# Gated feed-forward: square roots behind a step's evictions, attention's sums one group per step and three ahead, router and weighing in another order

## The chip, the cores and the metric
One core of a Trainium2 chip runs the whole program in one launch. The metric is device time in microseconds, the median of several runs. TensorE (PE) does the matrix products, VectorE (DVE) and ScalarE (ACT) the element-wise work, GpSimd (POOL) issues indirect transfers and SyncE (SP) plain ones.

## The reference, cut to what matters
A graph of 6250 nodes with 256 features passes through two message-passing layers and two feed-forward layers, each on the normalized rows and added to them. The change touches the second of the four:

```python
x = x + gnn0(layernorm(x), edge_attr, src, dst)                 # attention
x = x + ffn0(layernorm(x))                                      # this stage
x = x + gnn1(layernorm(x), src, dst)
x = x + ffn1(layernorm(x))

def ffn0(x):
    all_out = _experts_mlp(x, eW1, eb1, eW2, eb2, eW3, eb3)     # 4 experts, 256-128-64-256
    shared = _shared_mlp(x, sW1, sb1, sW2, sb2, sW3, sb3)       # 256-256-128-256
    gates = softmax(x @ gW + gb)
    topv, topi = top_k(gates, 2)
    topw = softmax(topv)
    gated = sum of the two chosen experts' outputs, weighed by topw
    return shared + gated
```

## The kernel before, in words
The program runs in phases; the function `gated_experts` is one of them, between attention and the second graph layer. It holds all rows in `GX` as 49 blocks of 128 rows and works on 25 groups of `GT` = 2 blocks (the last has one). Each engine has a hand-written list of work: `first` for the start and `rest` for every group g, unrolled, so each engine's order is the order of the code, and semaphores tie them.

Before a block can be used, attention's sums, which lie transposed in `ACC`, are added: PE transposes them into `pY` (`attended` on PE, L1982), DVE adds a bias (L1721) and `pY` (L1724) to the block. Then the block is normalized: `row_stats` (L243), `center` (the aggregates L1704 and the copy of the means L1706), a square root on ScalarE (`root`, L1902), its reciprocal on DVE (`scale`, L1739). Before the change sums are added in chunks of `YC` = 4 blocks, two chunks in `first` and one in each of the steps 0 to 10, and the roots are taken in five growing parts.

A step g then does, on PE: the first layers of the shared net (S1) and the experts (E1) from `xT`, in accumulations that rotate over three banks `pM`; `weights` (L2010, the transposition of the gate weights); `turn` (L1991, the transposition of the next group's rows); the second layers (S2, and the experts' `halves`, L2036); the spreading of the gate weights to `pW` (L2059) and the output's biases to `pO` (L2065); the next group's router `logits` (L2002); the last layers into `pO` (L2074, L2079). ScalarE evicts every accumulation with a bias and a Relu (`mid`, L1939), evicts `turn` into `xT` (L1884) and takes the exponentials of the router (L1891) and of the difference of its two best values (L1896). The roots and the exponentials use different function tables, and `ACT_TABLE_LOAD` brings one in.

DVE normalizes (`normed`, L1780), weighs (`weigh`, L1813 to L1819, then the copy of `wT`, L1823), multiplies the experts by their weights (`e2w`, L1853), picks the two best experts (`gates`, L1788 to L1806, nineteen small operations, with ScalarE's exponential in between) and adds the output to the block (L1862). The finished blocks are normalized once more for the next layer, in eight `pieces`: means and variances on DVE, a root (`kept`, L1908), `keep` (L1746, L1749, L1755), the scaled rows on ScalarE (`row_out`, L1917) or DVE, and POOL scatters them (L1693).

What sets the order around the change, on ScalarE at the head of a step before:

```python
for r in range(2, len(parts)):
    if g == chunk_end(r) - 1:
        root(r)
for n, (i0, i1) in enumerate(pieces):
    if i1 == g * GT:
        kept(n)
...
for n in range(KD):
    mid(n, h1[:, n, 0:w], B1[:, n:n + 1])
```

Of the kernel before, what the change touches and what calls it, by code (L numbers as in the profile page):

```python
# [21 lines left out]
ALU = mybir.AluOpType  # L22
# [22 lines left out]
PW = D + 3  # L45
# [1562 lines left out]
def gated_experts(nc, sb, ps, sem, sems, x, ACC, IDI, XND, F, x_in, bi_in, GX, ST, MEAN, RSTD, ident, iota, epsc, SORTD):  # L1608
# [3 lines left out]
    YC = 2 * GT  # L1612
    NY = (RB + YC - 1) // YC
    NGR = (RB + GT - 1) // GT
    parts = [(0, YC), (YC, 2 * YC), (2 * YC, 4 * YC), (4 * YC, 8 * YC), (8 * YC, RB)]
# [8 lines left out]
    def chunk_end(r):  # L1624
        return (parts[r][1] + YC - 1) // YC - 1

# [4 lines left out]
    with ExitStack() as s:  # L1631
# [20 lines left out]
        NMR = sb(s, "NMRk", [128, RB])  # L1652
        g_ = {n: sb(s, f"gate_{n}", [128, GT, NG]) for n in ("l", "p", "eq", "m1", "q", "w")}
# [19 lines left out]
        with nc.Block() as block:  # L1673
# [26 lines left out]
            def _(dve):  # L1700
# [8 lines left out]
                def attended(q, j):  # L1709

                    i0 = q * YC + j * GT
                    w = min(GT, RB - i0)
                    if w <= 0:
                        return
                    for n, (a, b) in enumerate(XPARTS):
                        if a == i0 or a == i0 + 1:
                            dve.wait_ge(x_in[n], 16 * (b - a))
                    if i0 == 0:
# [3 lines left out]
                    dve.wait_ge(yt_ready, i0 // GT + 1)  # L1722
# [12 lines left out]
                def scale(r):  # L1735

                    dve.wait_ge(r_ready, r + 1)
                    i0, i1 = parts[r]
                    nc.vector.reciprocal(RSTD[:, i0:i1], SD[0][:, i0:i1])  # L1739
                    dve.drain()  # L1740
# [67 lines left out]
                def weigh(g, k):  # L1808
                    w = width(g)
                    one = g_["w"][:, 0:w, :]  # L1810
                    dve.wait_ge(ex_ready, g * 2 + 2)

                    nc.vector.tensor_scalar(r_["f"][:, 0:w], r_["e"][:, 0:w], 1.0, None, ALU.add)  # L1813
                    nc.vector.tensor_tensor(one, one, spread(r_["e"], w), ALU.mult)
                    dve.drain()
                    nc.vector.reciprocal(r_["f"][:, 0:w], r_["f"][:, 0:w])
                    nc.vector.tensor_tensor(one, one, g_["m1"][:, 0:w, :], ALU.add)
                    dve.drain()
                    nc.vector.tensor_tensor(GWP[:, 0:w, 0:2, 0:NG], one.unsqueeze(2).to_broadcast([128, w, 2, NG]),  # L1819
                                            r_["f"][:, 0:w].unsqueeze(2).unsqueeze(3).to_broadcast([128, w, 2, NG]),  # L1820
                                            ALU.mult).then_inc(w_ready, 1)
                    dve.wait_ge(wt_ready, g + 1)
                    nc.vector.tensor_copy(wT[k][:, 0:w * 128], pG[0:WROW + NG + 1, 256:256 + w * 128]).then_inc(wt_copied, 1)  # L1823

                def first(g, k):
                    nc.vector.memset(GWP[:, :, :, :], 0.0)
                    nc.vector.tensor_scalar(IDE[:, :], iota[:, 0:NG], -1.0, float(NG), ALU.mult, ALU.add)
                    dve.drain()
                    nc.vector.memset(GWP[:, :, 1, NG], 1.0)
                    for j in range(2):  # L1830
                        attended(0, j)
                    measured(0)
                    scale(0)
                    normed(g)
                    gates(g)
                    for j in range(2):
                        attended(1, j)
                    measured(1)

                def rest(g, k, more):  # L1840
                    w = width(g)
                    for r in range(1, len(parts)):
                        if g == chunk_end(r):
                            scale(r)
                    if more:
                        normed(g + 1)
                    weigh(g, k)
                    if g + 2 < NY:
                        attended(g + 2, 0)
# [11 lines left out]
                    v = block_of(GX, g * GT, w)  # L1861
                    nc.vector.tensor_tensor(v, v, pO[:, 0:w * D].rearrange("p (m d) -> p m d", d=D), ALU.add).then_inc(o_read, 1)  # L1862
                    dve.drain()
                    for m in range(w):
                        row_stats(nc, ST, GX, g * GT + m, PW)
                    if g + 2 < NY:
                        measured(g + 2)
                    for n, (i0, i1) in enumerate(pieces):
                        if i1 == g * GT:
                            keep(n)  # L1870
                        if i1 == min((g + 1) * GT, RB):
                            dve.drain()
                            center(i0, i1, MV[1]).then_inc(kc_ready, 1)
                            if not more:
                                keep(n)
# [4 lines left out]
            def _(act):  # L1880
# [17 lines left out]
                def root(r):  # L1898

                    act.wait_ge(c_ready, chunk_end(r) + 1)  # L1900
                    i0, i1 = parts[r]
                    nc.scalar.activation(SD[0][:, i0:i1], MV[0][:, i0:i1, 1], ACT.Sqrt, bias=epsc[:, :]).then_inc(r_ready, 1)  # L1902

                def kept(n):

                    act.wait_ge(kc_ready, n + 1)
                    i0, i1 = pieces[n]
                    nc.scalar.activation(SD[1][:, i0:i1], MV[1][:, i0:i1, 1], ACT.Sqrt, bias=epsc[:, :]).then_inc(kr_ready, 1)  # L1908

# [12 lines left out]
                def first(g, k):  # L1922
                    root(0)
                    normed(g, k)
                    exp_gates(g)

                def rest(g, k, more):
                    w = width(g) * 128
                    for r in range(2, len(parts)):
                        if g == chunk_end(r) - 1:  # L1930
                            root(r)
                    for n, (i0, i1) in enumerate(pieces):
                        if i1 == g * GT:
                            kept(n)

# [18 lines left out]
                    if g == 0:  # L1954
                        root(1)
# [10 lines left out]
            def _(pe):  # L1966
# [6 lines left out]
                def attended(q, j):  # L1973

                    i0 = q * YC + j * GT
                    if i0 >= RB:
                        return
                    if i0:
                        pe.wait_ge(y_read, i0 // GT)
                    for m in range(min(GT, RB - i0)):  # L1980
                        for c in range(KD):
                            last = nc.tensor.transpose(pY[:, m * D + c * 128:m * D + (c + 1) * 128],  # L1982
                                                       acc[:, c, (i0 + m) * 128:(i0 + m + 1) * 128], ident[:, :])
                    last.then_inc(yt_ready, 1)
# [29 lines left out]
                def first(g, k):  # L2014
                    for j in range(2):
                        attended(0, j)
                    turn(g)
                    logits(g, k)
                    for j in range(2):
                        attended(1, j)  # L2020

                def rest(g, k, more):
# [16 lines left out]

                    if g + 2 < NY:  # L2040
                        attended(g + 2, 0)
# [5 lines left out]
                    if more:  # L2047
                        turn(g + 1)

# [17 lines left out]
                    if g + 2 < NY:  # L2067
# [620 lines left out]
```

## Time and profile before

| | before |
|---|---|
| median of 3 runs | 3106.71 us (3104.43 to 3108.81) |
| the profiled execution's own time | 3102.67 us |
| its span | 3100.9 us |
| busy: PE, DVE, ACT, POOL | 75%, 56%, 41%, 59% of the span |
| this stage, from its first to the next phase's first work | 1248.4 to 1701.2 us |
| busy in the stage: PE, DVE, ACT | 356.1, 232.9, 180.8 of 452.8 us |

The span is the time between the first and the last instruction of one profiled execution; the shares are means over phases with different limits, so the stage is read by itself. DVE's busy time counts its operations, not the drains between dependent ones.

### The profile page before, as it was taken

What the parts mean: (1) busy time and instruction counts of PE and PEld (TensorE: products, weight loads), DVE (VectorE), ACT (ScalarE), POOL (GpSimd) and SP (SyncE); (2) the same over time, 40 slices, a digit from 0 to 9 for tenths busy, and PEclk for the clock granted to TensorE, in tenths of its full rate; (3) what the DMA queues carried; (4) which work ended last, traced back from release to release, by engine and by line L of the source; (5) the groups of instructions that cost most, each with busy time, mean ns of one, the idle gap of its engine ahead of it and who ended that gap; (6) DMA issues with size and microseconds to landing.
All of it is one profiled execution on the core that took longest, in us unless ns stands there. A gap on an engine that the chain in (4) does not pass through costs nothing. (4 is left out here: it accounts for less than half of the span.)

```text
span 3100.9 us, 46865 instructions
## 1 busy us (share of the span) xinstructions
PE 2331.6 (75%) x12072; PEld 1959.1 (63%) x12072; DVE 1741.5 (56%) x5674; ACT 1273.4 (41%) x4542; POOL 1837.1 (59%) x1935
## 2 busy tenths in 40 slices
PE   5986667667666666688894787888888888875098
PEld 4876666666666566566773676666666666764087
DVE  5434888898888887566452433333333333476154
ACT  1534555555555444333543433333333333353033
POOL 5575777777777775501122777777777777400645
PEclk8998788888888878798996656555555556687599
DMA  7698444444444453600001333333333333203242
GB/s 208 178 230 218 110 111 112 113 112 111 113 113 111 113 128 85 207 1 14 14 28 36 106 106 106 106 106 106 106 106 106 106 106 106 66 1 53 99 140 83
DMA packets 250114, 323.65 MB, mean 104 GB/s; under 512 B 152723, under 2 KB 181001, under 8 KB 249335
## 3 DMA queue, kind: packets, MB, share of 16 engines
q0 software_dynamic: 89424, 235.59, 27.1%
q1 hardware_dynamic: 155784, 82.05, 11.1%
q10 hardware_dynamic: 4640, 3.02, 0.5%
q8 instruction: 100, 1.64, 0.2%
q14 instruction: 166, 1.36, 0.1%
HBM read 276.41 MB, written 48.24 MB: 105 GB/s over the span
## 5 line engine op out<-in xcount | busy, mean ns | idle before, releaser
L1526 PE MATMUL pAb<-HOTb,Gb 128*128 128x128 f32 x3136 | 840.8, 425 | 173.3 <-DMA Gb<-normed_rows,SRCT 122.0
L1505 POOL DMA_INDIRECT Gb<-normed_rows,SRCT x784 | 741.2, 945 | 248.9 <-issue 238.5
L1526 PEld LDWEIGHTS pAb<-HOTb,Gb 128*128 128x128 f32 x3136 | 659.7, 297 | 354.8 <-DMA Gb<-normed_rows,SRCT 273.9
L1566 DVE TENSOR_TENSOR ACC<-ACC,pAb 128x256 f32 x784 | 330.6, 422 | 641.7 <-PE pAb L1526 568.6
L1093 POOL DMA_INDIRECT GX<-ft_rows,SRCT x432 | 412.3, 954 | 131.5 <-issue 130.9
L1179 ACT ACTIVATE ACC<-apA 128x254 f32 x784 | 300.4, 383 | 411.5 <-PE apA L1252 339.9
L1252 PE MATMUL apA<-AHOT,GX 128*128 128x129 f32 x1920 | 304.8, 329 | 84.2 <-DVE GX L1401 84.2
L1252 PEld LDWEIGHTS apA<-AHOT,GX 128*128 128x128 f32 x1920 | 290.5, 241 | 101.9 <-DVE GX L1401 101.9
L1545 ACT ACTIVATE HOTb<-OFFb 128x1024 f32<-128x1024 f32 x98 | 103.6, 1057 | 604.1 <-PE pAb L1526 604.0
L1093 POOL DMA_INDIRECT G<-ft_rows,SRCT x288 | 274.6, 954 | 87.6 <-issue 85.4
L1693 POOL DMA_INDIRECT normed_rows<-nrow,IDI x49 | 48.1, 981 | 338.8 <-ACT nrow L1917 325.4
L1541 ACT ACTIVATE OFFb<-iota,NRELb 128x128 f32<-128x128 f32 x784 | 239.6, 388 | 6.9 <-issue 0.3
L1252 PE MATMUL apA<-AHOT,G 128*128 128x129 f32 x1216 | 197.9, 335 | 48.2 <-DVE G L1401 46.4
L1252 PEld LDWEIGHTS apA<-AHOT,G 128*128 128x128 f32 x1216 | 189.4, 247 | 59.0 <-DVE G L1401 56.9
L1401 DVE TENSOR_TENSOR GX<-GX,apV 128x1024 f32<-128x1024 f32 x120 | 143.1, 1192 | 0.0
L1180 ACT ACTIVATE FL<-apA 128x4 f32<-128x4 f32 x784 | 135.1, 172 | 0.0
L2298 POOL DMA_INDIRECT rows_by_expert<-GX,POSI x49 | 48.6, 992 | 135.5 <-DVE POSI L2485 120.9
L2029 PE MATMUL fpM<-fxT,ffn_E 128*128 128x256 f32 (+1 forms) x400 | 103.4, 414 | 33.5 <-ACT h L1939 33.5
L2546 POOL DMA_INDIRECT out_dram<-sO,sID x80 | 77.7, 972 | 76.2 <-issue 41.5
L1301 DVE TENSOR_TENSOR AHOT<-apL,RELT 128x1024 f32<-128x1024 f32 x98 | 118.6, 1210 | 0.0
L2029 PEld LDWEIGHTS fpM<-fxT,ffn_E 128*128 128x128 f32 x400 | 82.9, 213 | 49.8 <-ACT h L1939 37.3
L520 PE MATMUL pS<-VB,eT 128*128 128x128 f32 x784 | 97.7, 279 | 0.5 <-ACT V L617 0.5
(415 smaller groups left out, 3954.2 us busy)
## 6 DMA issues: line engine op xcount, KB each, us to landing
ebuf<-in_edge_attr_dram SPq DMA_DIRECT2D x49, 448.0 KB
Gb<-normed_rows,SRCT POOLq DMA_INDIRECT x784, 2.7
rows_by_expert<-ffn_PADT SPq DMA_DIRECT2D x1, 10360.0 KB, 44.8
sT<-rows_by_expert SPq DMA_DIRECT2D x80, 129.5 KB, 2.1
GX<-ft_rows,SRCT POOLq DMA_INDIRECT x480
ft_rows<-row SPq DMA_DIRECT2D x25, 231.0 KB
GX<-in_x_dram SPq DMA_DIRECT2D x10, 560.0 KB
G<-ft_rows,SRCT POOLq DMA_INDIRECT x304
```

Source lines behind the costliest of these rows:

```text
L1093: pool.indirect_dma_start(G[c % GS][:, m, :], None, FT[:, :], bass.IndirectOffsetOnAxis(ap=SRCT[:, t:t + 1], axis=0)).then_inc(g_in[c % GS ...
L1179: nc.scalar.activation(acc[:, :, ds(r + 1, EP - 1)], sums[:, :, 1:EP], ACT.Copy)
L1180: nc.scalar.activation(FL[:, :, f:n + 1:n - f], sums[:, :, 0:HW:EP], ACT.Copy).then_inc(pfree[b], 1)
L1252: last = nc.tensor.matmul(pA[b][:, f * HW:(f + 1) * HW], G[c % GS][:, m, f * 128:(f + 1) * 128], HOT[c % 2][:, m, :], start=True, stop=True)
L1301: nc.vector.tensor_tensor(HOT[c % 2][:, h * HT:(h + 1) * HT, 0:EP], pL[0:EP, 256:256 + EP].unsqueeze(1).to_broadcast([EP, HT, EP]), RELT[: ...
L1401: nc.vector.tensor_tensor(v, v, pV[0:EP, 0:128].rearrange("p (h m) -> p h m", m=UT)[:, :, m:m + WB].rearrange("p h m -> p m h").unsqueeze( ...
L1505: pool.indirect_dma_start(G[g % R][m][:, :], None, TABLE[:, :], bass.IndirectOffsetOnAxis(ap=SRCT[:, t:t + 1], axis=0)).then_inc(g_in[g % ...
L1526: last = nc.tensor.matmul(pA[b][:, o:o + EP], G[k][m][:, c * 128:(c + 1) * 128], HOT[k % 2][:, m, :], start=True, stop=True)
L1541: nc.scalar.activation(OFF[k2][:, m, :], iota[0:EP, 0:EP], ACT.Abs, bias=NREL[k2][:, m:m + 1])
L1545: nc.scalar.activation(HOT[k2][:, :, :], OFF[k2][:, :, :], ACT.Relu, bias=1.0, scale=-1.0).then_inc(hot[k2], 1)
L1566: last = nc.vector.tensor_tensor(acc[:, :, ds(b, EP)], acc[:, :, ds(b, EP)], pA[q][:, o:o + KD * EP].rearrange("p (c r) -> p c r", c=KD), ...
L2029: last = nc.tensor.matmul(pM[bank[n]][:, 0:w], one, v, start=(c == 0), stop=(c == len(pairs) - 1))
```

## The change
Attention's sums are added one group (two blocks) per step, with statistics, aggregates and the copy of the means at once; in step 0 the groups 2 and 3, in step g the group g + 3. The parts of the roots follow: one group, one group, then two groups each. The roots (`root`, `kept`) move from the head of a step on ScalarE to its end, behind the evictions and the next group's exponential, and a dummy exponential on one element (`exp_next`) follows them. The second exponential comes behind the first expert's eviction. On DVE weighing comes ahead of normalizing, the copy of `wT` is parted from it, the output is added at the end of a step and its statistics are taken in the next one (`settled`). On PE the sums' transposes and the logits move ahead of the experts' second layers.

The tables:

```diff
+    AHEAD = 3
+    parts = [(0, 1), (1, 2)] + [(g, min(g + 2, NGR)) for g in range(2, NGR, 2)]
+    coming = [[2, 3]] + [[g + AHEAD] if g + AHEAD < NGR else [] for g in range(1, NGR)]
```

On DVE:

```diff
-                def measured(q):
-
-                    i0, i1 = q * YC, min((q + 1) * YC, RB)
-                    dve.drain()
-                    for i in range(i0, i1):
+                    dve.drain()
+                    for i in range(i0, i0 + w):
                         row_stats(nc, ST, GX, i, PW)
                     dve.drain()
-                    center(i0, i1, MV[0]).then_inc(c_ready, 1)
+                    last = center(i0, i0 + w, MV[0])
+                    if any(q == b - 1 for a, b in parts):
+                        last.then_inc(c_ready, 1)
...
                 def rest(g, k, more):
                     w = width(g)
-                    for r in range(1, len(parts)):
-                        if g == chunk_end(r):
+                    weigh(g, k)
+                    for r, (a, b) in enumerate(parts):
+                        if a == g + 1:
                             scale(r)
                     if more:
                         normed(g + 1)
-                    weigh(g, k)
-                    if g + 2 < NY:
-                        attended(g + 2, 0)
+                    for n, (i0, i1) in enumerate(pieces):
+                        if i1 == (g - 1) * GT:
+                            keep(n)
+                    if g:
+                        settled(g - 1)
+                    dve.wait_ge(wt_ready, g + 1)
+                    nc.vector.tensor_copy(wT[k][:, 0:w * 128], pG[0:WROW + NG + 1, 256:256 + w * 128]).then_inc(wt_copied, 1)
+                    for q in coming[g]:
+                        attended(q)
...
-                    if g + 2 < NY:
-                        attended(g + 2, 1)
                     if more:
                         gates(g + 1)
-                    dve.wait_ge(o_ready, g + 1)
...
+                    else:
+                        keep(len(pieces) - 2)
+                    added(g)
+                    if not more:
+                        settled(g)
+                        keep(len(pieces) - 1)
```

On ScalarE:

```diff
                 def rest(g, k, more):
                     w = width(g) * 128
-                    for r in range(2, len(parts)):
-                        if g == chunk_end(r) - 1:
-                            root(r)
-                    for n, (i0, i1) in enumerate(pieces):
-                        if i1 == g * GT:
-                            kept(n)
...
-                        if e == 1:
+                        if e == 0:
                             exp_second(g)
...
                     if more:
                         exp_gates(g + 1)
-                    else:
+                    due = 0
+                    for r, (a, b) in enumerate(parts):
+                        if r >= 2 and b - 1 in coming[g]:
+                            root(r)
+                            due += 1
+                    for n, (i0, i1) in enumerate(pieces):
+                        if i1 == g * GT:
+                            kept(n)
+                            due += 1
+                    if not more:
                         kept(len(pieces) - 1)
+                    elif due:
+                        exp_next()
```

On PE:

```diff
-                    if g + 2 < NY:
-                        attended(g + 2, 0)
...
                     weights(g)
                     if more:
                         turn(g + 1)
+                    for q in coming[g][0:1]:
+                        attended(q)
...
                     mid(KD + NG, [(S2[:, c, :], h1[:, c, 0:w]) for c in range(KD)])
+                    pe.wait_ge(wt_copied, g + 2)
+                    if more:
+                        logits(g + 1, 1 - k)
                     for b in range(NB):
                         halves(KD + NG + 1 + b, b)
-                    pe.wait_ge(wt_copied, g + 2)
...
-                    if g + 2 < NY:
-                        attended(g + 2, 1)
-                    if more:
-                        logits(g + 1, 1 - k)
+                    for q in coming[g][1:2]:
+                        attended(q)
```

How the instructions stand before and after, engine by engine (line, operation, output <- inputs, shape, how many in a row). ScalarE around a root of the kept rows, before:

```order
L1939 ACTIVATE e<-fpM,ffn_C 128x256 x2
L1891 ACTIVATE gate_p<-gate_l 128x8
L1908 ACT_TABLE_LOAD
L1908 ACTIVATE SDm<-MVm,epsc 128x8
L1939 ACTIVATE h<-fpM,ffn_B 128x256 x2
L1939 ACTIVATE e<-fpM,ffn_C 128x256 x2
L1896 ACT_TABLE_LOAD
L1896 ACTIVATE gred_e<-gred_d 128x2
L1939 ACTIVATE e<-fpM,ffn_C 128x256 x2
```

and around a root now:

```order
L1939 ACTIVATE e<-fpM,ffn_C 128x256 x2
L1893 ACTIVATE gate_p<-gate_l 128x8
L1904 ACT_TABLE_LOAD
L1904 ACTIVATE SDm<-MVm,epsc 128x4
L1914 ACT_TABLE_LOAD
L1914 ACTIVATE spare<-epsc 128x1
L1939 ACTIVATE h<-fpM,ffn_B 128x256 x2
L1939 ACTIVATE e<-fpM,ffn_C 128x256
L1898 ACTIVATE gred_e<-gred_d 128x2
```

The load and the root stood ahead of the first evictions (`h`, `e`), with a second load inside the evictions; now load, root, load and dummy stand behind the next group's exponential (`gate_p`), and the second exponential (`gred_e`) comes one eviction earlier.

DVE from the adding of a group's output to the copy of `wT`, before (step 1 to step 2):

```order
L1862 TENSOR_TENSOR GX<-GX,fpO 128x2x256
L243 BN_STATS ST<-GX 128x6 x6
L1704 BN_AGGR MVm<-ST 128x2 x4
L1706 COPY MEAN<-MVm 128x4
L1780 TENSOR_SCALAR fxn<-GX,MEAN,RSTD 128x256 x2
L1813 TENSOR_SCALAR gred_f<-gred_e 128x2
L1814 TENSOR_TENSOR gate_w<-gate_w,gred_e 128x8
L1816 RECIPROCAL gred_f<-gred_f 128x2
L1817 TENSOR_TENSOR gate_w<-gate_w,gate_m 128x8
L1819 TENSOR_TENSOR gate_rows<-gate_w,gred_f 128x2x2x4
L1823 COPY wT<-fpG 37x256
```

and now (from step 0 into step 1, up to the first add of attention's sums):

```order
L1824 TENSOR_TENSOR GX<-GX,fpO 128x2x256
L1809 TENSOR_SCALAR gred_f<-gred_e 128x2
L1810 TENSOR_TENSOR gate_w<-gate_w,gred_e 128x8
L1812 RECIPROCAL gred_f<-gred_f 128x2
L1813 TENSOR_TENSOR gate_w<-gate_w,gate_m 128x8
L1815 TENSOR_TENSOR gate_rows<-gate_w,gred_f 128x2x2x4
L1735 RECIPROCAL RSTD<-SDm 128x4
L1776 TENSOR_SCALAR fxn<-GX,MEAN,RSTD 128x256 x2
L243 BN_STATS ST<-GX 128x6 x2
L1861 COPY wT<-fpG 37x256
L1719 TENSOR_TENSOR GX<-GX,ffn_BI 128x2x256
```

The statistics of six blocks and four aggregates between the output and the weighing are gone from there; the weighing (L1813 to L1819 before, L1809 to L1815 now) follows the output directly, and normalizing and two statistics come behind it.

PE from the first layers to the logits, before:

```order
L2029 MATMUL fpM<-fxT,ffn_S 128x256 x4
L2029 MATMUL fpM<-fxT,ffn_E 128x256 x8
L2010 MATMUL fpG<-ident,gate_rows 128x128 x2
L1991 MATMUL fpT<-ident,fxn 128x128 x4
L2029 MATMUL fpM<-h,ffn_S 128x256 x2
L2036 MATMUL fpM<-e,ffn_E 64x256 x4
L2059 MATMUL fpW<-wT,ffn_SEL 128x256
L2065 MATMUL fpO<-ffn_OB,wT 128x256
L2059 MATMUL fpW<-wT,ffn_SEL 128x256
L2065 MATMUL fpO<-ffn_OB,wT 128x256
L1982 MATMUL fpY<-ident,ACC 128x128 x4
L2002 MATMUL fpG<-ffn_GW,fxT 128x128 x4
```

and now:

```order
L2034 MATMUL fpM<-fxT,ffn_S 128x256 x4
L2034 MATMUL fpM<-fxT,ffn_E 128x256 x8
L2017 MATMUL fpG<-ident,gate_rows 128x128 x2
L1998 MATMUL fpT<-ident,fxn 128x128 x4
L1989 MATMUL fpY<-ident,ACC 128x128 x4
L2034 MATMUL fpM<-h,ffn_S 128x256 x2
L2009 MATMUL fpG<-ffn_GW,fxT 128x128 x4
L2041 MATMUL fpM<-e,ffn_E 64x256 x4
L2066 MATMUL fpW<-wT,ffn_SEL 128x256
L2072 MATMUL fpO<-ffn_OB,wT 128x256
L2066 MATMUL fpW<-wT,ffn_SEL 128x256
L2072 MATMUL fpO<-ffn_OB,wT 128x256
```

The sums' transposes (`fpY`) and the logits (`fpG<-ffn_GW,fxT`) stood behind the spreading of the gate weights (`fpW`); now they stand ahead of the experts' second layers.

## Rows read from the trace of the kernel before
**Rows 1.** Windows: stretch, its us, busy us (records) per engine, granted clock, DMA, GB/s.
```profile
1292.30:1664.40 372.10, 320.29 (x1674) 251.09 (x1674) 203.57 (x885) 161.92 (x343) 41.13 (x41) 0.93 0.05 16
1350.20:1365.80 15.60, 13.64 (x79) 10.89 (x78) 11.31 (x46) 5.78 (x14) 0.00 (x0) 1.00 0.00 0
1401.80:1424.20 22.40, 16.60 (x76) 12.50 (x77) 11.90 (x53) 7.95 (x16) 0.00 (x0) 0.77 0.00 0
1506.10:1518.80 12.70, 12.70 (x71) 10.02 (x71) 6.55 (x31) 6.21 (x14) 2.88 (x3) 1.00 0.12 43
1586.60:1603.40 16.80, 14.35 (x74) 10.96 (x73) 7.53 (x40) 8.87 (x18) 0.00 (x0) 0.95 0.00 1
```

**Rows 2.** Waits from 1292.3 to 1664.4: who waited, total us, times, longest.
```profile
ACT SDm L1908 <- DVE MEAN L1706: 39.5, 7, 7.2
```

**Rows 3.** Timeline (start us, us, engine, line, operation, count, idle before), step with a root.
```profile
1419.39 0.30 ACT L1908 ACTIVATE SDm<-MVm,epsc 128x8 f32<-128x8 f32 x1 [7.20 <-DVE MEAN L1706]
1420.10 4.80 PE L2029 MATMUL fpM<-fxT,ffn_E 128*128 128x256 f32 x12 [5.01 <-ACT h L1939]
1422.71 1.28 ACT L1896 ACT_TABLE_LOAD   x1
1424.00 0.20 ACT L1896 ACTIVATE gred_e<-gred_d 128x2 f32<-128x2 f32 x1
```

**Rows 4.** Timeline of PE: sums' transposes at 1428, then a step without roots or sums.
```profile
1428.83 0.66 PE L1982 MATMUL fpY<-ident,ACC 128*128 128x128 f32 x4
1429.32 1.06 PE L2002 MATMUL fpG<-ffn_GW,fxT 128*128 128x128 f32 x8
1506.92 0.44 PE L2010 MATMUL fpG<-ident,gate_rows 128*128 128x128 f32 x2
1508.76 1.08 PE L2036 MATMUL fpM<-e,ffn_E 128*64 128x256 f32 x8
1509.77 0.48 PE L2059 MATMUL fpW<-wT,ffn_SEL 4*128 4x256 f32 x1
1510.84 1.16 PE L2002 MATMUL fpG<-ffn_GW,fxT 128*128 128x128 f32 x8
1514.42 1.89 PE L2029 MATMUL fpM<-fxT,ffn_S 128*128 128x256 f32 x8
```

**Rows 5.** Timeline of DVE and ScalarE: aggregates at 1417, then that same step.
```profile
1417.76 0.38 DVE L1704 BATCH_NORM_AGGREGATE MVm<-ST 128x2 f32<-128x6 f32 x4
1506.08 0.17 DVE L1813 TENSOR_SCALAR gred_f<-gred_e 128x2 f32<-128x2 f32 x1
1507.40 0.42 DVE L1823 COPY wT<-fpG 37x256 f32<-37x256 f32 x1 [0.53 <-PE fpG L2010]
1510.94 0.69 DVE L1853 TENSOR_TENSOR e2w<-e,fpW 128x512 f32<-128x512 f32 x1 [3.12 <-PE fpW L2059]
1512.03 0.17 DVE L1788 TENSOR_TENSOR gate_l<-fpG,ffn_GBB 128x8 f32<-128x8 f32 x1 [0.41 <-PE fpG L2002]
1512.72 0.21 ACT L1891 ACTIVATE gate_p<-gate_l 128x8 f32<-128x8 f32 x1 [1.08 <-DVE gate_l L1793]
1515.49 0.47 ACT L1939 ACTIVATE h<-fpM,ffn_B 128x256 f32<-128x256 f32 x1 [2.56 <-PE fpM L2029]
1516.76 0.68 DVE L1862 TENSOR_TENSOR GX<-GX,fpO 128x512 f32<-128x512 f32 x1
1517.53 0.75 DVE L243 BATCH_NORM_STATS2 ST<-GX 128x6 f32<-128x256 f32 x2
1518.20 0.72 DVE L1780 TENSOR_SCALAR fxn<-GX,MEAN,RSTD 128x256 f32<-128x256 f32 x2
```

**Rows 6.** Timeline of PE and POOL: the stage's first and last work.
```profile
1258.64 2.07 PE L2002 MATMUL fpG<-ffn_GW,fxT 128*128 128x128 f32 x8 [0.69 <-ACT fxT L1884]
1269.52 3.62 PE L2029 MATMUL fpM<-fxT,ffn_S 128*128 128x256 f32 x8
1690.53 0.97 POOL L1693 DMA_INDIRECT normed_rows<-nrow,IDI  x1 [0.30 <-issue]
```

More of the change, by code:

```diff
@@ L1622, in gated_experts, with rows_of @@
             kept_in.setdefault(i1 // GT + 1 + (i - i0) // 2, []).append((n, i))
-    def chunk_end(r):
-        return (parts[r][1] + YC - 1) // YC - 1
+    def rows_of(a, b):
+        return slice(a * GT, min(b * GT, RB))
     def out_before(n):
@@ L1707, in center, with attended @@
                     return last
[L1709 to L1714, printed above, removed]
+                def attended(q):
+                    i0, w = q * GT, width(q)
                     for n, (a, b) in enumerate(XPARTS):
-                        if a == i0 or a == i0 + 1:
+                        if a == i0:
                             dve.wait_ge(x_in[n], 16 * (b - a))
-                    if i0 == 0:
+                    if q == 0:
                         dve.wait_ge(bi_in, 16)
@@ L1821, in weigh, with added, settled @@
                                             ALU.mult).then_inc(w_ready, 1)
-                    dve.wait_ge(wt_ready, g + 1)
-                    nc.vector.tensor_copy(wT[k][:, 0:w * 128], pG[0:WROW + NG + 1, 256:256 + w * 128]).then_inc(wt_copied, 1)
+                def added(g):
+                    w = width(g)
+                    dve.wait_ge(o_ready, g + 1)
+                    v = block_of(GX, g * GT, w)
+                    nc.vector.tensor_tensor(v, v, pO[:, 0:w * D].rearrange("p (m d) -> p m d", d=D), ALU.add).then_inc(o_read, 1)
+                    dve.drain()
+                def settled(g):
+                    for m in range(width(g)):
+                        row_stats(nc, ST, GX, g * GT + m, PW)
+                    for n, (i0, i1) in enumerate(pieces):
+                        if i1 == min((g + 1) * GT, RB):
+                            dve.drain()
+                            center(i0, i1, MV[1]).then_inc(kc_ready, 1)
                 def first(g, k):
@@ L1829, in first @@
                     nc.vector.memset(GWP[:, :, 1, NG], 1.0)
-                    for j in range(2):
-                        attended(0, j)
-                    measured(0)
+                    attended(0)
                     scale(0)
                     normed(g)
+                    attended(1)
                     gates(g)
-                    for j in range(2):
-                        attended(1, j)
-                    measured(1)
                 def rest(g, k, more):
                     w = width(g)
-                    for r in range(1, len(parts)):
-                        if g == chunk_end(r):
+                    weigh(g, k)
+                    for r, (a, b) in enumerate(parts):
+                        if a == g + 1:
                             scale(r)
@@ L1898, in root @@
                 def root(r):
-                    act.wait_ge(c_ready, chunk_end(r) + 1)
-                    i0, i1 = parts[r]
-                    nc.scalar.activation(SD[0][:, i0:i1], MV[0][:, i0:i1, 1], ACT.Sqrt, bias=epsc[:, :]).then_inc(r_ready, 1)
+                    act.wait_ge(c_ready, r + 1)
+                    o = rows_of(*parts[r])
+                    nc.scalar.activation(SD[0][:, o], MV[0][:, o, 1], ACT.Sqrt, bias=epsc[:, :]).then_inc(r_ready, 1)
                 def kept(n):
@@ L1908, in kept, with exp_next @@
                     nc.scalar.activation(SD[1][:, i0:i1], MV[1][:, i0:i1, 1], ACT.Sqrt, bias=epsc[:, :]).then_inc(kr_ready, 1)
+                def exp_next():
+                    nc.scalar.activation(spare[:, :], epsc[:, :], ACT.Exp)
                 def row_out(n, i):
@@ L1923, in first @@
                     root(0)
+                    root(1)
                     normed(g, k)
@@ L1928, in rest @@
                     w = width(g) * 128
-                    for r in range(2, len(parts)):
-                        if g == chunk_end(r) - 1:
-                            root(r)
-                    for n, (i0, i1) in enumerate(pieces):
-                        if i1 == g * GT:
-                            kept(n)
                     def mid(n, to, b):
@@ L1959, in rest @@
                         exp_gates(g + 1)
-                    else:
+                    due = 0
[3 more added lines that the diff above has]
+                            due += 1
+                    for n, (i0, i1) in enumerate(pieces):
+                        if i1 == g * GT:
+                            kept(n)
+                            due += 1
+                    if not more:
                         kept(len(pieces) - 1)
+                    elif due:
+                        exp_next()
                 unrolled(NGR, 2, lambda c, k, i: first(c, k), lambda c, k, i, more: rest(c, k, more))
@@ L1971, in _, with attended @@
                 pe.sem_inc(wt_copied, 1)
[L1973 to L1980, printed above, removed]
+                def attended(q):
+                    if q:
+                        pe.wait_ge(y_read, q)
+                    for m in range(width(q)):
                         for c in range(KD):
+                            i = q * GT + m
                             last = nc.tensor.transpose(pY[:, m * D + c * 128:m * D + (c + 1) * 128],
-                                                       acc[:, c, (i0 + m) * 128:(i0 + m + 1) * 128], ident[:, :])
+                                                       acc[:, c, i * 128:(i + 1) * 128], ident[:, :])
                     last.then_inc(yt_ready, 1)
@@ L2014, in first @@
                 def first(g, k):
-                    for j in range(2):
-                        attended(0, j)
+                    for q in range(2):
+                        attended(q)
                     turn(g)
                     logits(g, k)
-                    for j in range(2):
-                        attended(1, j)
                 def rest(g, k, more):
```

25 lines of the change are left out of this document (5 added, 20 removed).

## The prediction
> **What bounds the kernel now.** I read the windows first. The change touches one stage, the gated feed-forward, whose 25 groups of two row blocks are handled in 25 steps. I cut it where DVE begins the weighing of a group (the division by 1 + e, L1813): from the second group's weighing to the last one's are 372.1 us, that is 23 steps, 16.18 us each [rows 1]. TensorE is recorded busy for 320.3 us of that, so it looks like the bound. The windows of single steps say otherwise: a step that carries neither square roots nor attention's sums takes 12.70 us, and in it PE is busy for all of 12.70; one with roots alone takes 16.80; one with two groups of sums and no roots 15.60; one with both 22.40, at a granted clock of 0.77. PE sets only the 12.70. What is above it is waiting.
>
> Where the waiting is stands in the table of waits and the timeline. In these 23 steps ScalarE sat 39.5 us, seven times, in front of the square roots of L1908 alone until DVE had finished its means [rows 2]. ScalarE runs in order, and the evictions of the next accumulations stand behind the root. The timeline shows one: the root starts at 1419.39 after 7.20 us, and PE, out of banks, starts again at 1420.10 after 5.01 us, for 12 records that take 4.80 us, 0.40 each, where eight take 1.89, 0.24 each, at the full clock [rows 3, 4]. Then the exponential of the router's second value needs its table again (1.28 us) before DVE can weigh. The kernel alternates: DVE holds ScalarE, ScalarE holds PE, PE comes back at half speed, and DVE waits for all of them.
>
> **The root.** It now stands behind the last evictions of a step and the exponential of the next group, in the gap before the next step's first accumulation is ready, and it works on sums added three groups ahead, finished in the same step before e2w. So it waits for nothing. A dummy exponential behind it fetches the other table. I cost its place by the fast step [rows 4, 5]. PW (the spreading of the gate weights, 1509.77) starts 1.17 us before e2w (1510.94); e2w takes 0.69; the exponential ends 0.90 after the router's first instruction (1512.03 to 1512.93). Two loads, the root and the dummy are 1.28 + 0.30 + 1.28 + 0.20 = 3.06. ScalarE is free 1.17 + 0.69 + 0.90 + 3.06 = 5.82 us after PW starts. PE reaches the next accumulations 4.65 after PW (1514.42), minus 0.99 for the logits that move ahead of PW, so at 3.66, and two accumulations take 1.89. The first is ready at 4.6; it is evicted 1.2 late. But PE has three banks: the fourth accumulation, at 3.66 + 2.8 = 6.5, needs the first bank, read by 5.82 + 0.47 = 6.29. Two evictions take 0.94 and two accumulations 1.89, so ScalarE catches up. Cost: zero to 0.4 us; its cover is these three banks. Without it, a root costs its lateness of 1.2 us.
>
> Here a rule speaks against the change. The trace: the load begun at 1422.71 ends at 1423.99 and the exponential starts at 1424.00 [rows 3]; nothing is drained behind a load. The Trainium skill (ScalarE: Activation LUTs, What ACT_TABLE_LOAD costs, and its table-set sections) says to group functions by set, since a switch is about 1.28 us of load plus 1.38 of drain; the change goes from 25 loads to 29. By that page the pair above would be 2.76 us longer. The trace denies the drain, so I leave it out of the sum.
>
> **Attention's sums.** The same 49 blocks, but one group per step in steps 1 to 21 (two in step 0) instead of two in steps 0 to 10. On DVE one group is two adds (0.68, or 0.77 with the drain behind: 1516.76 to 1517.53), two statistics (0.75), two aggregates (four take 0.38) and a small copy (0.16, as L1813), with drains between of under 0.1 each: 2.7 to 2.9 us [rows 5]. On PE it is four transposes, recorded as 0.66, though the next matmuls start 0.49 after them (1428.83 to 1429.32); the same overlap of 0.17 makes the logits 0.99 of their 1.16 [rows 4].
>
> **The step's three loops.** (a) PE: the step in which it is never idle, 12.70 [rows 1], plus 0.49 to 0.66: 13.2 to 13.4. (b) DVE alone: weighing 0.84, normalizing 0.72, statistics 0.75, copy of wT 0.42, sums 2.8, e2w 0.69, gates 4.73 (1512.03 to 1516.76), adding 0.77: 11.7, and 0.3 more on average for scales, shifts and kept means. (c) Through both: weighing to PE's transposition 0.84 (1506.08 to 1506.92); up to 0.5 in which PE now waits for the normalized rows, since these come behind the weighing instead of ahead of it; transposition to PW 2.85 plus the moved transposes 0.49 to 0.66 and logits 0.99 to 1.16; PW to e2w 1.17; e2w 0.69; gates 4.73; adding 0.77. Sum 13.03 to 13.37, or 12.5 if PE is late enough not to wait for the rows. The copy of wT, behind the normalizing and statistics, ends about 2.8 after the weighing began, or 3.7 with eight kept means; PE asks for it after its second shared layer, at about 0.84 + 0.5 + 1.84 (1506.92 to 1508.76) = 3.2, plus up to 0.5 for the transposes: it waits at most 0.5, once in four steps. I take 13.3 for all: (a) and (c) nearly tie, and the odd 0.4 for a root or a late copy lies between their ends. In steps 22 and 23 no sums are left: 12.7.
>
> 23 steps: 21 x 13.3 + 2 x 12.7 = 304.7 instead of 372.1, a gain of 67.4.
>
> **Head and tail.** Now PE's first accumulations start at 1269.52, although the logits were done by 1260.71; between lie transposes that wait for DVE's sums [rows 6]. The change moves them off that path: 8.8 us earlier. Step 0 adds two groups of sums now as before, and I leave its length. In the last step six blocks are scaled (as normalizing, two in 0.72 [rows 5]: 2.2 us) ahead of the copy of wT, on which the last evictions and so the last kept rows wait; behind these POOL issues the scatters up to 1690.53. A loss of 2.2. The edits of pieces (spans of parts, the second exponential one eviction earlier) move nothing else.
>
> Sum: 8.8 + 67.4 - 2.2 = 74.0. The profiled execution took 3102.67 us; the median of the three runs, 3106.71, is 4.04 above. On the median: 3106.7 - 74 = 3032.7, rounded to **3032 us**.
>
> **Rivals.**
> *Roots still bite* (0.14). Something I don't see makes ScalarE later by two more loads' worth, 2.6 us, in each of the 12 root steps of the loop (g = 0, 2 ... 20, and 21): 31 us, 3063. For: three banks are all the cover, and steps with a root and a kept root have another 0.30. Against: the 0.01 between load and exponential. The Trainium skill's drain, above, would be this case.
> *DVE remains the pace* (0.10). Its waits stay additive, as in today's 15.60 step with sums and no roots, where PE is busy for only 13.64: 21 x 15.6 instead of 21 x 13.3 is 48 more, 3081. Against: that step carries two groups, and DVE's own sum is 11.7.
> *Slower* (0.04). The second exponential now stands behind the first expert's eviction, not the second's. If DVE finishes the gates later than that, ScalarE holds three experts' evictions, PE runs out of banks and its clock falls, as at 1420.10. It decides from the point where a step exceeds (372.1 + 6.6 - 25.4) / 21 = 16.8 us, 3.5 above my loop; at 18 us a step the time is 3107 + 25 = 3132. Against: the gates end 1.17 + 0.69 + 4.73 = 6.59 after PW starts, and that eviction ends at 3.66 + 2.8 + 0.47 = 6.9 at the earliest; behind it there are again three banks.
> My forecast has 0.72.
>
> **Range.** The forecast's own: 12.9 instead of 13.3 takes 8 off, a head better by 6 another 6: 3018; at 14.15, halfway between 12.70 and 15.60, 18 more: 3050. To hold 8 in 10 I take in the roots' case with a margin: **3015 to 3068**; left out are DVE's pace and the slower case. 0.2% is 6 us, about what a measurement of this kernel can tell from no change. Faster 0.95, same 0.02, slower 0.03: all but the slower case lie well below, and that case can end on either side of its point.
>
> **What would show it.** Right: steps of 13 to 13.5 us, alike whether they have roots or not; no wait of a root on DVE's means; PE's waits on evictions below 1 us and a granted clock of 1.00 in the loop; the second weighing at about 1283 and the last at about 1588. Wrong: PE idle behind ScalarE's evictions after root steps (first rival); e2w starting late with PE idle before the last matmuls, or DVE without idle time (second); ScalarE waiting for DVE in front of the second exponential (third).

## The result and the profile after

The changed kernel takes 3021.99 us (median of 4 runs, 3016.28 to 3026.84) against 3105.57 of before on the same chip: a ratio of 0.973 [0.971, 0.975], faster by 83.6 us. The forecast was 3032 us, 74 less. The profiled execution took 3018.93 us, its span 3017.1, 83.8 under that of before.

Windows of the changed kernel, with the columns of [rows 1] (the busy columns are PE, PE's weight loads, DVE, ScalarE, POOL): the 23 steps from the second weighing to the last one, a step behind a root, and the next one, which has a root at its end.

```profile
1280.50:1577.70 297.20, 295.64 (x1689) 242.98 (x1689) 208.11 (x909) 172.26 (x368) 51.84 (x50) 1.00 0.10 33
1436.20:1449.20 13.00, 13.00 (x76) 10.82 (x75) 9.55 (x41) 6.21 (x14) 4.72 (x5) 1.00 0.14 50
1449.20:1462.10 12.90, 12.90 (x75) 10.69 (x75) 9.06 (x38) 9.06 (x18) 0.00 (x0) 1.00 0.01 2
```

The 372.10 of [rows 1] are 297.20: 12.92 a step, alike with and without roots, PE busy in 99.5% of them at a granted clock of 1.00. Of the 74.9 us, 50.2 are idle time of PE (51.8 before, 1.6 now) and 24.7 are busy time (320.3 before, 295.6 now), as the granted clock rose from 0.93 to 1.00. Waits of the changed kernel from 1270 to 1610, as in [rows 2]:

```profile
DVE e2w L1867 <- PE fpW L2066: 33.9, 24, 4.1
ACT SDm L1910 <- DVE MEAN L1707: 12.7, 1, 12.7
DVE gred_f L1809 <- ACT gred_e L1898: 7.6, 22, 0.4
PE fpM L2034 <- ACT h L1939: 1.0, 2, 0.8
PE fpM L2041 <- DVE wT L1861: 2.2, 1, 2.2
```

The one wait of a root on means that is left is that of the very last piece, behind which no eviction stands. DVE waits for PE now, and no step's PE waits over 1 us for an eviction. The timeline from a root (L1904, L1910, the kept rows' of the same table) to the turn answers to [rows 3]:

```profile
1431.66 1.28 ACT L1904 ACT_TABLE_LOAD   x1
1432.74 1.89 PE L2034 MATMUL fpM<-fxT,ffn_S 128*128 128x256 f32 x8
1432.96 0.30 ACT L1904 ACTIVATE SDm<-MVm,epsc 128x4 f32<-128x4 f32 x1
1433.16 0.28 ACT L1910 ACTIVATE SDm<-MVm,epsc 128x8 f32<-128x8 f32 x1
1433.46 1.28 ACT L1914 ACT_TABLE_LOAD   x1
1434.47 3.77 PE L2034 MATMUL fpM<-fxT,ffn_E 128*128 128x256 f32 x16
1434.76 0.20 ACT L1914 ACTIVATE spare<-epsc 128x1 f32<-128x1 f32 x1
1434.87 0.82 ACT L1939 ACTIVATE h<-fpM,ffn_B 128x256 f32<-128x256 f32 x2
1435.94 0.21 ACT L1898 ACTIVATE gred_e<-gred_d 128x2 f32<-128x2 f32 x1
1437.13 0.95 DVE L1776 TENSOR_SCALAR fxn<-GX,MEAN,RSTD 128x256 f32<-128x256 f32 x2
1438.29 0.60 PE L1998 MATMUL fpT<-ident,fxn 128*128 128x128 f32 x4
```

Two loads, two roots and the dummy run while PE accumulates; the evictions start at 1434.87, and PE goes on at 0.24 us a record without a wait. The second exponential needs no load. The stage's head and end in the timeline, to be read beside [rows 6]:

```profile
1259.94 3.45 PE L2034 MATMUL fpM<-fxT,ffn_S 128*128 128x256 f32 x8
1264.66 0.20 ACT L1898 ACTIVATE gred_e<-gred_d 128x2 f32<-128x2 f32 x1
...
1582.11 0.66 PE L2041 MATMUL fpM<-e,ffn_E 128*64 128x128 f32 x8 [2.22 <-DVE wT L1861]
1605.65 0.97 POOL L1694 DMA_INDIRECT normed_rows<-nrow,IDI  x1 [0.30 <-issue]
```

The sum by the same cuts: the second weighing comes 12.3 us earlier against the stage's first transfer, the 23 steps take 74.9 less, the end from the last weighing to the last scatter 1.9 more (27.97 instead of 26.1). That is 85.3; the rest of the program is 1.5 longer.

### The profile page after: what moved, and what is told of

It is laid out like the page before. It is cut to its first block and busy times, and to the rows that moved or that the text cites. A ratio compares the mean times of both kernels' runs of the same rounds, so it can differ in the third digit from the quotient of the medians.

```text
span 3017.1 us, 46958 instructions
## 1 busy us (share of the span) xinstructions
PE 2261.7 (75%) x12072; PEld 1908.8 (63%) x12072; DVE 1745.5 (58%) x5695; ACT 1283.2 (43%) x4568; POOL 1837.4 (61%) x1935
## 5 line engine op out<-in xcount | busy, mean ns | idle before, releaser
L1526 PE MATMUL pAb<-HOTb,Gb 128*128 128x128 f32 x3136 | 811.5, 412 | 203.9 <-DMA Gb<-normed_rows,SRCT 154.0
L1526 PEld LDWEIGHTS pAb<-HOTb,Gb 128*128 128x128 f32 x3136 | 633.5, 286 | 382.3 <-DMA Gb<-normed_rows,SRCT 297.5
L2618 ACT ACTIVATE sxT<-spT 128x256 f32<-128x256 f32 x80 | 30.7, 383 | 164.5 <-PE spT L2566 164.5
L1159 ACT ACTIVATE ACC<-VAL 128x2 f32 x792 | 89.8, 196 | 11.9 <-ACT FL L1180 10.8
```

Source lines behind the costliest of these rows:

```text
L1526: last = nc.tensor.matmul(pA[b][:, o:o + EP], G[k][m][:, c * 128:(c + 1) * 128], HOT[k % 2][:, m, :], start=True, stop=True)
```

## The experiments

Each is an edit of the changed kernel, run beside the kernel before. Steps are the distances between weighings, from the timeline; the root of a step stands at its end.

**The sums two groups per step again** (steps 0 to 11, then none).

```diff
-    coming = [[2, 3]] + [[g + AHEAD] if g + AHEAD < NGR else [] for g in range(1, NGR)]
+    coming = [[q for q in (2 * g + 2, 2 * g + 3) if q < NGR] for g in range(NGR)]
```

> The changed kernel with attention's sums two groups per step again (steps 0 to 11 instead of one per step to step 21), everything else as changed: roots behind the gates, fresh sums still finished before e2w. Theory (PE sets 12.94 us a step because one group fits beside it): the second group's transposes come behind the spreading of the gate weights, so e2w starts about 2.6 us later; steps 1 to 10 at 15.1 to 15.6 as the changed kernel's step 0 (15.58), steps 12 to 21 0.4 shorter: 17 to 22 us slower than the changed kernel, about 3040. Rival (the roots alone gave the gain, spreading the sums none): same as changed, 3022.

3054.92 us, 0.984 [0.981, 0.987]: 33 above the changed kernel, beyond what was expected. Most steps with sums take 17.2, those without 12.8. Its timeline, in one step with sums, then windows of two such steps:

```profile
1383.84 0.17 DVE L1809 TENSOR_SCALAR gred_f<-gred_e 128x2 f32<-128x2 f32 x1 [2.02 <-ACT gred_e L1898]
...
1391.41 0.69 DVE L1722 TENSOR_TENSOR GX<-GX,fpY 128x512 f32<-128x512 f32 x1 [1.55 <-PE fpY L1989]
1393.50 0.69 DVE L1867 TENSOR_TENSOR e2w<-e,fpW 128x512 f32<-128x512 f32 x1
1394.24 3.55 PE L2084 MATMUL fpO<-ffn_E,e2w 128*128 128x256 f32 x8 [2.07 <-DVE e2w L1867]
```

```profile
1401.15:1418.41 17.26, 15.24 (x80) 12.29 (x79) 12.14 (x54) 9.48 (x19) 6.87 (x7) 0.90 0.13 47
1418.41:1433.97 15.56, 13.55 (x80) 11.02 (x79) 11.71 (x47) 9.07 (x18) 0.98 (x1) 1.00 0.05 17
```

The second group's sums push e2w back, PE waits 2.07 us for it, and its next eight records take 3.55 instead of 1.89. The wait alone makes a step of 15.56, as expected, in the two steps that keep a granted clock of 1.00. The other eight, at 0.90, take 1.7 us more each; without these 14 us the run would be 19 above, as expected. The roots come in every step here, with six table loads more, and PE waits for no eviction in these steps. Within the changed kernel, adding one group per step is worth 33 us.

**The sums' means reported late**, behind the output's add, so that the root waits again.

```diff
-                    if any(q == b - 1 for a, b in parts):
+                    if q < 4 and any(q == b - 1 for a, b in parts):
...
+                    if any(q >= 4 and q == b - 1 for q in coming[g] for a, b in parts):
+                        dve.sem_inc(c_ready, 1)
```

> The changed kernel, but DVE signals the sums' variances to ScalarE only after it has added the step's output, as late as a root of before had to wait. Nothing else moves. Theory (it is the root's wait, not its place, that cost): in each of the 11 or 12 root steps ScalarE is free about 2.8 us later than now, the three banks are already used up, so 2.5 to 3.5 us a root step: 28 to 42 us slower than changed, 3050 to 3064, with PE waiting for evictions after each root. Rival (the gain came from the spreading and the order): within 6 us of changed.

3069.86 us, 0.988 [0.987, 0.990]: 48 above, more than the expected 28 to 42. Waits from 1283 to 1560, then windows ahead of one idle time of PE (1433.15 to 1435.75), behind it, and of the whole next step:

```profile
ACT SDm L1906 <- DVEq L1825: 26.7, 9, 3.2
PE fpM L2036 <- ACT h L1941: 25.2, 9, 3.1
```

```profile
1430.40:1433.20 2.80, 2.75 (x13) 2.09 (x11) 2.06 (x12) 0.20 (x1) 0.00 (x0) 1.00 0.00 0
1435.75:1440.30 4.55, 4.55 (x14) 3.68 (x15) 2.13 (x10) 1.71 (x5) 0.00 (x0) 0.62 0.00 0
1436.55:1451.23 14.68, 14.68 (x77) 12.01 (x77) 9.15 (x39) 6.21 (x14) 0.00 (x0) 0.91 0.00 0
```

A wait of 3 us of a root is a wait of 3 us of PE. Steps with a root take 15.7 to 16.2, those behind them mostly 14.7: both suffer, for different reasons. In the first PE is idle. In the second it is busy throughout, but after the 2.60 us of idle time it came back at a granted clock of 0.62, and the whole next step has 0.91.

**Two more loads and dummies per root step**, with no wait.

```diff
-                    nc.scalar.activation(spare[:, :], epsc[:, :], ACT.Exp)
+                    nc.scalar.activation(spare[:, 0:1], epsc[:, :], ACT.Exp)
+                    nc.scalar.activation(spare[:, 1:2], epsc[:, :], ACT.Sqrt)
+                    nc.scalar.activation(spare[:, 2:3], epsc[:, :], ACT.Exp)
```

> The changed kernel with a second dummy pair (root and exponential on one element, two more table loads) behind each root: ScalarE free 2 x (1.28 + 0.20) = 2.96 us later in 12 steps, nothing waited for. Theory (cover of three banks is about used up by one pair): 2 to 3 us a root step, 24 to 36 us slower than changed, 3046 to 3058. Rival (ScalarE has room, catches up between evictions): within 6 us of changed.

3081.94 us, 0.993 [0.991, 0.995]: 60 above, twice what was expected, with steps like those of the late means. Timeline, then the wait for evictions in the 23 steps, then two steps that stand behind a root:

```profile
1430.84 1.28 ACT L1916 ACT_TABLE_LOAD   x1
1432.13 0.20 ACT L1916 ACTIVATE spare<-epsc 128x1 f32<-128x1 f32 x1
1432.24 0.82 ACT L1941 ACTIVATE h<-fpM,ffn_B 128x256 f32<-128x256 f32 x2
1432.75 2.86 PE L2036 MATMUL fpM<-fxT,ffn_E 128*128 128x256 f32 x12 [2.69 <-ACT h L1941]
```

```profile
PE fpM L2036 <- ACT h L1941: 35.1, 12, 3.8
```

```profile
1403.12:1417.80 14.68, 14.68 (x76) 11.97 (x75) 9.43 (x40) 6.22 (x14) 2.09 (x2) 0.88 0.08 28
1433.55:1446.55 13.00, 13.00 (x76) 10.83 (x75) 9.11 (x39) 6.21 (x14) 0.00 (x0) 1.00 0.00 0
```

The addition is 2 x (1.28 + 0.20) = 2.96 us, PE's idle time 2.69: the three banks had hardly 0.3 us of cover left. So a root's wait has no effect of its own; lateness of ScalarE beyond that cover does, whatever makes it late. The idle time adds up to 35.1 us, as expected. Most of the rest is the clock: behind an idle time the next step takes 14.68 us at a granted clock of 0.88 without any idle time, and 13.00 in the one place where the clock stayed at 1.00.

**No dummy exponential.**

```diff
-                    elif due:
-                        exp_next()
```

> The changed kernel without the dummy exponential: the second table load of a root step falls between the first expert's eviction and the second exponential, 1.28 us. Theory: weighing starts 1.3 to 1.4 us later in 12 steps; PE reaches the weights' transposition 1.1 us after they are ready, so 0.2 to 0.5 us of it show: 3 to 6 us slower than changed, hardly to be told from none. Rival (the dummy carries much of the gain): the whole 1.28 or more shows, 15 us and above.

3034.26 us, 0.976 [0.974, 0.979]: 12 above, where 3 to 6 were expected. Steps with a root take 14.3, the others 12.7. Timeline:

```profile
1445.80 1.28 ACT L1898 ACT_TABLE_LOAD   x1
1447.10 0.20 ACT L1898 ACTIVATE gred_e<-gred_d 128x2 f32<-128x2 f32 x1
1447.33 0.17 DVE L1809 TENSOR_SCALAR gred_f<-gred_e 128x2 f32<-128x2 f32 x1 [1.77 <-ACT gred_e L1898]
1448.23 0.44 PE L2015 MATMUL fpG<-ident,gate_rows 128*128 128x128 f32 x2 [0.37 <-DVE gate_rows L1815]
1449.19 0.66 PE L1996 MATMUL fpT<-ident,fxn 128*128 128x128 f32 x4 [0.52 <-DVE fxn L1776]
```

The expectation took the slack of the gate rows, 1.1 us; the normalized rows, which stand behind the weighing now, have only 0.2 behind a root (done at 1438.08, turned at 1438.29 in the changed kernel). PE waits for both, 0.37 and 0.52 us here, and most of the load shows: 309.7 us in the 23 steps instead of 297.2, about 1.1 a root.

**The three old orders together** (the edits of the next three).

> The changed kernel with the three small orders of before: normalizing ahead of weighing, logits behind the spreading of the gate weights, the second exponential behind the second expert's eviction. Sums and roots as changed. Theory (PE sets the step and reaches the transposition of the gate weights 1.1 us after they are ready): weighing 0.9 to 1.1 us later, all of it inside that slack: 0 to 5 us slower than changed, steps still 12.9 to 13.1. Rival (the orders carry part of the gain): 0.5 to 1 us in each of 24 steps, 12 to 24 us slower.

3012.59 us, 0.969 [0.966, 0.972]: 8 *below* the changed kernel run beside it (3020.47, the last run below). The new orders were not needed. Window over 21.5 steps:

```profile
1283.00:1560.00 277.00, 276.95 (x1588) 226.27 (x1588) 198.62 (x850) 161.34 (x342) 47.22 (x48) 1.00 0.10 33
```

PE has no idle time. The next three runs ask which order costs.

**Only the logits late:**

```diff
-                    pe.wait_ge(wt_copied, g + 2)
-                    if more:
-                        logits(g + 1, 1 - k)
                     for b in range(NB):
                         halves(KD + NG + 1 + b, b)
+                    pe.wait_ge(wt_copied, g + 2)
...
                     for q in coming[g][1:2]:
                         attended(q)
+                    if more:
+                        logits(g + 1, 1 - k)
```

> The changed kernel with one old order: PE's logits (and with them the wait for the copy of wT) behind the spreading to pW again, the rest new. With all three old orders it was 8 us faster than the changed kernel: 2.8 of it lies between the last weighing and the next phase, the rest in step 0 (0.9), the last step (0.8) and some tenths in the steps between. Theory A, the logits' place is what costs: in the last step the experts' second layers no longer wait for the copy of wT, so the tail gives 2.8 back, and PE's second layers stand closer to the first; 5 to 8 us faster than the changed kernel, about 3014. Theory B, normalizing behind the weighing is what costs: only the tail's 2.8 comes back, about 3018. Theory C, the second exponential's place costs: 2.8 here as well.

3013.91 us, 0.971 [0.969, 0.973]: 8 below the 3021.99, 6.6 below the second measurement of the changed kernel (3020.47). It is theory A. Step 0 takes 14.7 instead of 15.6: there the second group's sums stood behind the logits. The last step takes 11.6 instead of 12.1, and from the last weighing to the next phase 36.4 instead of 38.7, since the last experts' layers no longer wait for wT.

**Only the normalizing ahead of the weighing** (`weigh(g, k)` moved behind `normed(g + 1)`).

> The changed kernel with one old order: DVE normalizes ahead of the weighing again, the rest new. Theory A, the logits' place is what costs: no difference to the changed kernel within 2 us, about 3021. Theory B, PE waits some tenths a step for the normalized rows because they stand behind the weighing: the turn's wait of 0.2 to 0.4 us goes in part of the steps, 3 to 5 us faster, about 3017. Theory C: no difference.

3022.58 us, 0.973 [0.972, 0.975]: no difference.

**Only the second exponential behind the second expert** (`if e == 1:`).

> The changed kernel with one old order: the second exponential behind the second expert's eviction again, the rest new. The weighing then starts one eviction (0.43 us) later. Theory A: on PE the weights' transposition has 1.1 us of slack, the normalized rows behind the weighing 0.2, so up to 0.2 us a step lost in 24 steps: 0 to 5 us slower, about 3023. Theory B: since the normalized rows stand behind the weighing, all of it shows: 5 to 10 us slower, about 3029. Theory C, the early place holds back an eviction that PE waits for: 3 to 5 us faster, about 3017.

3038.67 us, 0.979 [0.977, 0.981]: 17 above, more than any theory gave. Steps take 13.3 to 14.1. Timeline:

```profile
1440.95 0.17 DVE L1809 TENSOR_SCALAR gred_f<-gred_e 128x2 f32<-128x2 f32 x1 [1.21 <-ACT gred_e L1898]
1442.45 0.66 PE L1998 MATMUL fpT<-ident,fxn 128*128 128x128 f32 x4 [0.18 <-DVE fxn L1776]
```

The weighing waits 1.21 us instead of 0.39 and the normalized rows behind it hold up PE, in 20 steps out of 20 from 1285 to 1560. With normalizing first (the old orders, where the logits are late as well) the late place costs nothing: the early exponential pays only for the other new order.

**The fifth piece's rows earlier:** four blocks a step in steps 21 and 22.

```diff
-            kept_in.setdefault(i1 // GT + 1 + (i - i0) // 2, []).append((n, i))
+            kept_in.setdefault(i1 // GT + 1 + (i - i0) // (4 if n == NPA - 1 else 2), []).append((n, i))
```

> The changed kernel with the last ScalarE piece of finished rows (blocks 32 to 39) written four blocks a step in steps 21 and 22 instead of two a step in steps 21 to 24. POOL's last 17 scatters then do not all start behind the last step: 8 of them run during it. Theory: POOL ends with the last 9, the last block's chain sets the end, 10 to 15 us faster than changed, about 3009. Rival (two more scalings a step make ScalarE late and PE waits): no gain.

3007.19 us, 0.968 [0.965, 0.971]: 13 below the changed kernel run beside it, as expected. In the changed kernel POOL had been idle for 39.6 us when these rows came, and then its queue of scatters, 1.28 us each, set the end.

**This and the old orders together.**

> The two faster versions together: the three old orders, and piece 4 of the kept rows scaled four blocks a step in steps 21 and 22. With the old orders alone the kernel was 8 us faster than the changed one, with the early rows alone 13.3. Theory A, the gains lie in different places (the old orders in the steps and in the wait for the copy of wT, the early rows in the queue of scatters behind the last step): 18 to 22 us faster, 2999 to 3004. Rival: both shorten the same end, which the scatters then bound, so only the larger and the steps' 3 to 5 count: 3004 to 3007.

2998.81 us (2996.76 to 3002.99), 0.966 [0.965, 0.968]: 23 below the changed kernel and faster than both. The gains add, as in theory A. Its timeline, in which the next phase starts 24.73 us after the last weighing (1573.95) instead of 38.67:

```profile
1587.98 0.97 POOL L1694 DMA_INDIRECT normed_rows<-nrow,IDI  x1 [0.30 <-issue]
1598.68 0.37 SPq L1495 DMA_DIRECT2D WMEAN<-in_L_gnn_W_src_dram  x1
```

**The changed kernel again**, beside the old orders and the early rows, with no edit.

> The changed kernel itself, beside the next two on the same chip: 3016 to 3027, a span of 3015 to 3025 us.

3020.47 us (3018.95 to 3022.98): 1.5 from its first median.

## Why the prediction was right, point by point

**The bound and the root: right.** The waits of [rows 2] are gone and every step is PE's. "Cost: zero to 0.4 us; its cover is these three banks" holds: steps with and without roots are alike to 0.1 us on the mean (13.0 and 12.9), and the estimate of the cover (banks needed at 6.5, free at 6.29, so 0.2) is what the doubled loads showed: 2.96 added, 2.69 of PE idle. One thing was put wrongly: the root did not move "behind the last evictions", since on ScalarE the end of one step and the head of the next adjoin; load and root stood behind gate_p before as well, as the listings show. What the change did was to make their inputs ready (sums three ahead; kept rows' roots a step later) and to fetch the table back with the dummy. The late means show the first, for the sums' roots, as worth 48 us, the missing dummy the second as worth 12. Not tried alone: the later place of the kept rows' roots, in front of which the 39.5 us of [rows 2] were, and the statistics taken a step later.

**The load: right, and it decides nothing here.** With 29 loads the chip shows 1.28 us of load and no drain: 1433.46 + 1.28 = 1434.74, the dummy at 1434.76. The drain of 1.38 us that the Trainium skill (ScalarE: Activation LUTs, What ACT_TABLE_LOAD costs) states is in no row of this case. The Trainium skill's advice to group functions by table set (ScalarE: Activation LUTs, Table sets: the hidden batching unit) does hold where the cover is gone: two loads and dummies more per root cost 60 us in all.

**The loop: the mechanism right, the size 7.5 us off.** The step that failed is "(a) PE: the step in which it is never idle, 12.70 [rows 1], plus 0.49 to 0.66: 13.2 to 13.4". Measured: 12.9 with sums, 12.8 without, in the old orders too. The sums' four transposes thus lengthen PE's step by 0.1, not by their start-to-start distance. The timeline of the changed kernel shows why, in a step with sums and in one without:

```profile
1451.18 0.60 PE L1998 MATMUL fpT<-ident,fxn 128*128 128x128 f32 x4
1451.62 0.60 PE L1989 MATMUL fpY<-ident,ACC 128*128 128x128 f32 x4
1452.06 1.03 PE L2034 MATMUL fpM<-h,ffn_S 128*128 128x256 f32 x4
...
1554.81 0.47 ACT L1939 ACTIVATE e<-fpM,ffn_C 128x256 f32<-128x256 f32 x1 [0.39 <-PE fpM L2034]
1554.82 0.60 PE L1998 MATMUL fpT<-ident,fxn 128*128 128x128 f32 x4
1555.54 1.10 PE L2034 MATMUL fpM<-h,ffn_S 128*128 128x256 f32 x4
```

Behind the turn the code makes PE wait until the last expert's accumulation is evicted. Without sums the second layers start 0.72 us after the turn, 0.26 behind that eviction's end at 1555.28; with sums they start 0.88 after it, and are recorded 0.07 shorter. Most of the sums' transposes thus fill a pause that PE has without them.

**The head: 12.3 instead of 8.8.** S1 starts 9.6 us earlier (1259.94 against 1269.52) in a stage that starts 0.4 later: 10.0. The second exponential follows S1 after 4.72 us instead of 6.19: 1.5 that was set to nothing. Of it 0.9 is the one eviction by which it stands earlier, 0.6 the earlier start of the first expert's eviction (4.35 us behind S1 instead of 4.96). Step 0 took 15.6 instead of 16.4. **The tail: 1.9 instead of 2.2**, by the predicted wait (2.22 us for the copy of wT). Against the forecast's gain the loop is 7.5 better, the head 3.5 and the tail 0.3, the rest of the program 1.5 worse: 9.8 in the profiled spans (83.8 instead of 74.0). So the forecast is not near by errors that cancel.

**The rivals.** *Roots still bite* is real as a mechanism, but needs 0.3 us more than there was. *DVE remains the pace* is near to what two groups per step do: 15.6 as in the rival where the granted clock stays at 1.00, 17.2 where it does not. *Slower*, by the earlier second exponential, had its sign wrong: placed late, with the weighing first, it costs 17 us. Not seen at all: that the logits' new place costs 7 to 8 us by the medians; 5.2 of it can be seen between the first weighing and the next phase (2.9 in the steps, 2.3 behind them).

## What to carry to other kernels

Before a load or a wait on an in-order engine is called hidden, count what the engine behind it can still do in its free banks: here 0.3 us was left, and 3 us more per root cost 48 to 60 us in 12 places, since the step grew by the idle time of PE and its successor by a lower granted clock. When a change bundles several new orders, look at each alone and all undone together: one of three paid only for another, and one cost 5 to 8 us. An end bound by one queue (here 1.28 us per scatter) is shortened by feeding that queue earlier.

## What the hardware showed beyond expectation

Idle times of 2.0 to 3.2 us on PE were mostly followed by a lower granted clock: behind nine of ten such steps with the late means (steps 2 to 20), behind nine of ten with the doubled loads, in eight of ten steps with two groups. One case of each kind: 0.62 for 4.55 us (the late means: 2.60 idle, 12 records in 4.54), and no fall (the doubled loads: 2.69 idle, 12 records in 2.86). As a mean over its two levels (1.2 and 2.4 GHz), 0.62 is mostly the lower one; what decides between the two cases stays open. Two normalizing operations of DVE took 0.95 us at 1437.13, where they take 0.72 in [rows 5]; why was not tried.
